# Second layer's expert weights: spread over partitions by transfers from memory, with rings of four buffers

## The reference, cut to what matters

```
combine[t, e] = routed weight of expert e for token t (8 of 64 are non-zero)
routed = sum over e of  combine[t, e] * ( relu(x @ up_w[e])^2 @ down_w[e] )     # 64 experts, 128 -> 64 -> 128
shared = relu(x @ shared_up_w)^2 @ shared_down_w                                # 128 -> 256 -> 128
out    = routed + shared
```

## Time and profile before

| | |
|---|---|
| median of 3 runs | 4811.27 us (4810.74 to 4814.55) |
| profiled execution, its own time | 4804.09 us |
| its span, first to last instruction | 4802.3 us |
| share of the span PE is busy | 76% |
| experts' phase of the second layer, first matmul to last sum | 2185.4 to 2784.8 us |

### The profile page before, as it was taken

The page is one execution under the profiler, slowest core; times in us unless marked ns, Lnnn a source line. Parts: engine busy times, 40 slices in busy tenths (PEclk is TensorE's granted clock), DMA queues, the critical chain, the costliest instruction groups (busy, mean ns, idle before and its releaser), DMA issues. The chain is left out here.

```text
span 4802.3 us, 104516 instructions
## 1 busy us (share of the span) xinstructions
PE 3656.9 (76%) x36852; PEld 2186.3 (46%) x36852; DVE 2650.2 (55%) x5988; ACT 1930.0 (40%) x3735; POOL 1159.8 (24%) x1804
## 2 busy tenths in 40 slices
PE   4699999489956999519999933456447539999997
PEld 1244444257732222216666621135446426666665
DVE  5577777511145777465555564743443546666664
ACT  4366666223323777312222212221102235655553
POOL 0111111000000111004656621600001524444441
PEclk9799999679977999759999966566557859999999
DMA  3322222000003111000000001011000323333331
GB/s 99 72 58 56 57 56 55 6 9 14 5 14 67 46 45 45 4 1 16 13 15 15 15 22 45 30 57 30 4 4 3 53 75 115 114 111 115 116 116 31
DMA packets 179869, 219.27 MB, mean 46 GB/s; under 512 B 36509, under 2 KB 154852, under 8 KB 179182
## 3 DMA queue, kind: packets, MB, share of 16 engines
q1 hardware_dynamic: 175470, 206.76, 15.0%
q0 software_dynamic: 4096, 8.40, 1.2%
HBM read 162.16 MB, written 34.60 MB: 41 GB/s over the span
## 5 line engine op out<-in xcount | busy, mean ns | idle before, releaser
L716 DVE TENSOR_REDUCE att_mx<-att_pS 128x1 f32<-128x512 f32 (+4 forms) x960 | 730.5, 787 | 289.9 <-PE att_pS L587 187.2
L679 ACT ACTIVATE att_E<-att_pX,att_gs 128x512 f32<-128x512 f32 (+3 forms) x1024 | 723.3, 740 | 409.6 <-PE att_pX L613 176.8
L582 PE MATMUL att_pS<-att_ks,att_qs 72*128 72x512 bf16 (+4 forms) x1536 | 409.3, 339 | 80.9 <-DMA att_ks<-parts 57.6
L1841 POOL TENSOR_TENSOR att_E<-att_E,att_rz 128x128 f32<-128x128 f32 (+3 forms) x512 | 357.5, 719 | 437.3 <-DVE att_rz L2049 437.3
L607 PE MATMUL att_pX<-att_qs,att_ks 75*128 75x512 bf16 (+4 forms) x1536 | 421.3, 329 | 30.4 <-ACT att_E L679 15.5
L1533 POOL TENSOR_TENSOR pairs_h<-pairs_c,pairs_r 128x512 f32<-128x512 f32 x272 | 344.2, 1269 | 189.8 <-DVE pairs_c L1593 189.3
L1580 ACT ACTIVATE pairs_r<-pairs_ph 128x512 f32<-128x512 f32 x272 | 162.5, 597 | 437.1 <-PE pairs_pc L1551 435.5
L1593 DVE TENSOR_TENSOR pairs_c<-pairs_pc,pairs_r 128x512 f32<-128x512 f32 x272 | 188.2, 692 | 253.2 <-ACT pairs_r L1580 248.8
L624 PE MATMUL att_pO<-att_E,att_vs 128*9 128x512 f32 (+3 forms) x3072 | 322.4, 492 | 1.3 <-ACT att_E L679 1.3
L545 POOL CAST att_mp<-att_m 16x128 bf16<-16x128 f32 x288 | 80.5, 279 | 942.0 <-DVE att_m L727 916.8
L1559 PEld LDWEIGHTS pairs_po<-pairs_a,pairs_h 128*128 128x128 f32 x2176 | 285.8, 192 | 41.2 <-POOL pairs_h L1533 2.2
(11 more groups left out here) (423 smaller groups left out, 6745.6 us busy)
## 6 DMA issues: line engine op xcount, KB each, us to landing
att_bias<-in_bias_dram SPq DMA_DIRECT2D x64, 896.0 KB, 4.5
parts<-proj_part SPq DMA_DIRECT2D x144, 128.0 KB, 2.3
att_xb<-xnT SPq DMA_DIRECT2D x64, 256.0 KB, 2.7
att_qs<-parts SPq DMA_DIRECT2D x192, 64.0 KB
att_ks<-parts SPq DMA_DIRECT2D x192, 64.0 KB
att_w<-in_w3a_dram SPq DMA_DIRECT2D x64, 192.0 KB, 2.4
att_qs<-parts SPq DMA_DIRECT2D x96, 96.0 KB
att_ks<-parts SPq DMA_DIRECT2D x96, 96.0 KB
```

Source lines behind the costliest of these rows:

```text
L582: ins = nc.tensor.matmul(pS[:, bank, n * w:(n + 1) * w], qs[:K1, u, x, q * P:(q + 1) * P], ks[:K1, u, x, :w], start=(n == 0 or not causal) ...
L679: nc.scalar.activation(E[:, kt % 2, WIDE * xp:WIDE * (xp + 1), :w], places(c)[0], ACT.Exp, scale=gs[:, g % 2, gain_of:gain_of + 1]).then_i ...
L716: V.reduce_max(dst, src, AX.X).then_inc(s_mx, 1)
L1841: nc.gpsimd.tensor_tensor(E[:, k, :width(j)], E[:, k, :width(j)], rz[:, u, k:k + 1].broadcast_to([P, width(j)]), ALU.mult).then_inc(s_n, 1)
```

## The change

A new phase, `spread_phase`, takes the place of "one1", "turn1a" and "turn1b". It turns `comb` itself in float32, copies it to on-chip memory with ACT, and writes it to a table in memory, `cT`: 68 rows of 4096 tokens, row e the weight of expert e, and four rows of ones for the shared part. `pairs_phase` then loads, for each pair, the row of its first expert onto partitions 0 to 63 and the row of its second onto 64 to 127, in two transfers: each reads one row of 16 KB 64 times and is 1 MB at its destination. The table `sel` and its cast, `cA`, `cB` and the two bf16 matmuls are gone. DVE computes `m` = relu(`ph`) * `c` in one instruction with `ph` from PSUM and `c` from the loaded rows, and POOL `h` = `m` * `r`. The rings `ph`, `po`, `r`, `m` and `h` have four buffers, and PE and DVE run three iterations ahead instead of two. SP issues four transfers for a pair, and PE and DVE wait for all four at the pair's first block.

```diff
+def spread_phase(nc, R, name, comb, NE, cT):
+    ROWS = cT.shape[0]
+        wt = p.sb("wt", [ROWS, B * T])
+        pt = p.ps("pt", [P, 2, T])
+            @block.sync
+            def _(sp):
+                sp.wait_ge(s_one, 1)
+                sp.dma_start(cT[NE:, :], wt[NE:, :]).then_inc(s_out, 16)
+                for n in range(B):
+                    sp.wait_ge(s_wt, n + 1)
+                    sp.dma_start(cT[:NE, n * T:(n + 1) * T], wt[:NE, n * T:(n + 1) * T]).then_inc(s_out, 16)
+                sp.wait_ge(s_out, 16 * (B + 1))
+            @block.vector
+            def _(dve):
+                nc.vector.memset(wt[NE:, :], 1.0).then_inc(s_one, 1)
+                nc.vector.memset(R.f[:, :, :], 0.0)
+            @block.tensor
+            def _(pe):
+                for n in range(B):
+                    if n >= 2:
+                        pe.wait_ge(s_wt, n - 1)
+                    for q in range(QT):
+                        ins = nc.tensor.transpose(pt[:NE, n % 2, q * P:(q + 1) * P], comb[:, n * QT + q], R.ident[:, :])
+                    ins.then_inc(s_t, 1)
+            @block.scalar
+            def _(act):
+                for n in range(B):
+                    act.wait_ge(s_t, n + 1)
+                    nc.scalar.activation(wt[:NE, n * T:(n + 1) * T], pt[:NE, n % 2], ACT.Copy).then_inc(s_wt, 1)
...
+    RING, AHEAD = 4, 3
...
-                        for k, src in enumerate((w1, w2, sel)):
-                            dst = a[:, v, k] if k < 2 else a[:, v, 2:].rearrange("p k f -> p (k f)")
-                            sp.dma_start(dst, src[bass.ds(e, 1), :, :].rearrange("o p f -> (o p) f")).then_inc(s_w[v], 16)
+                        for k, src in enumerate((w1, w2)):
+                            sp.dma_start(a[:, v, k], src[bass.ds(e, 1), :, :].rearrange("o p f -> (o p) f")).then_inc(s_w[v], 16)
+                        for k in range(2):
+                            sp.dma_start(c[k * HALF_P:(k + 1) * HALF_P, v], cT[bass.ds(e * 2 + k, 1), :].broadcast_to([HALF_P, B * T])).then_inc(s_w[v], 16)
...
-                        nc.gpsimd.tensor_tensor(h[:, g % 2], c[:, g % 2], r[:, g % 2], ALU.mult).then_inc(s_h, 1)
+                        nc.gpsimd.tensor_tensor(h[:, g % RING], m[:, g % RING], r[:, g % RING], ALU.mult).then_inc(s_h, 1)
...
-                        nc.tensor.matmul(ph[:, g % 2], a[:, v, 0], R.xnT[:, b * T:(b + 1) * T], start=True, stop=True)
-                        nc.tensor.matmul(pc[:, g % 2], sb_[:, v, 0], cA[:, b * T:(b + 1) * T], start=True, stop=False)
-                        nc.tensor.matmul(pc[:, g % 2], sb_[:NC, v, 1], cB[:, b * T:(b + 1) * T], start=False, stop=True).then_inc(s_up, 1)
+                        if b == 0:
+                            pe.wait_ge(s_w[v], at(64, 64 * (g // IT + 1)))
+                        if not (first and g < RING):
+                            pe.wait_ge(s_r, at(IT, g + 1 - RING))
+                            pe.wait_ge(s_m, at(IT, g + 1 - RING))
+                        nc.tensor.matmul(ph[:, g % RING], a[:, v, 0], R.xnT[:, b * T:(b + 1) * T], start=True, stop=True).then_inc(s_up, 1)
...
-                        nc.vector.tensor_tensor(c[:, g % 2], pc[:, g % 2], r[:, g % 2], ALU.mult).then_inc(s_c, 1)
+                        nc.vector.scalar_tensor_tensor(out=m[:, g % RING], in0=ph[:, g % RING], scalar=0.0, in1=c[:, v, b * T:(b + 1) * T],
+                                                       op0=ALU.max, op1=ALU.mult).then_inc(s_m, 1)
```

More of the change, by code:

```diff
@@ L1487, in pairs_phase @@
+def pairs_phase(nc, R, name, NPAIR, w1, w2, cT):
+    RING, AHEAD = 4, 3
+    HALF_P = P // 2
+    with phase(nc, name) as p:
+        a = p.sb("a", [P, 2, 2, P])
+        c = p.sb("c", [P, 2, B * T])
+        r = p.sb("r", [P, RING, T])
+        m = p.sb("m", [P, RING, T])
+        h = p.sb("h", [P, RING, T])
+        ph = p.ps("ph", [P, RING, T])
+        po = p.ps("po", [P, RING, T])
         s_w = [p.sem("w0"), p.sem("w1")]
-        s_sel = p.sem("sel")
         s_up = p.sem("up")
         s_r = p.sem("r")
-        s_c = p.sem("c")
+        s_m = p.sem("m")
@@ L1515, in body @@
                     at = At(pool, i)
[L1517 to L1524, removed]
-                    for g in range(IT):
[L1526 to L1532, removed]
-                        nc.gpsimd.tensor_tensor(h[:, g % 2], c[:, g % 2], r[:, g % 2], ALU.mult).then_inc(s_h, 1)
+                    for g in range(IT):
+                        pool.wait_ge(s_r, at(IT, g + 1))
+                        pool.wait_ge(s_m, at(IT, g + 1))
+                        if not (first and g < RING):
+                            pool.wait_ge(s_o, at(IT, g + 1 - RING))
+                        nc.gpsimd.tensor_tensor(h[:, g % RING], m[:, g % RING], r[:, g % RING], ALU.mult).then_inc(s_h, 1)
                 run_bodies(pool, NBODY, body)
@@ L1555, in down @@
                         pe.wait_ge(s_h, at(IT, g + 1))
-                        if not (first and g < 2):
-                            pe.wait_ge(s_f, at(IT, g - 1))
+                        if not (first and g < RING):
+                            pe.wait_ge(s_f, at(IT, g + 1 - RING))
                         for q in range(QT):
-                            ins = nc.tensor.matmul(po[:, g % 2, q * P:(q + 1) * P], h[:, g % 2, q * P:(q + 1) * P], a[:, v, 1], start=True, stop=True)
+                            ins = nc.tensor.matmul(po[:, g % RING, q * P:(q + 1) * P], h[:, g % RING, q * P:(q + 1) * P], a[:, v, 1], start=True, stop=True)
                         ins.then_inc(s_o, 1)
                     if first:
-                        up(0, True)
-                        up(1, True)
+                        for g in range(AHEAD):
+                            up(g, True)
                     for g in range(IT):
-                        if not (last and g + 2 >= IT):
-                            up(g + 2, first)
+                        if not (last and g + AHEAD >= IT):
+                            up(g + AHEAD, first)
                         down(g, first)
@@ L1577, in body @@
                         act.wait_ge(s_up, at(IT, g + 1))
-                        if not (first and g < 2):
-                            act.wait_ge(s_h, at(IT, g - 1))
-                        nc.scalar.activation(r[:, g % 2], ph[:, g % 2], ACT.Relu).then_inc(s_r, 1)
+                        if not (first and g < RING):
+                            act.wait_ge(s_h, at(IT, g + 1 - RING))
+                        nc.scalar.activation(r[:, g % RING], ph[:, g % RING], ACT.Relu).then_inc(s_r, 1)
                 run_bodies(act, NBODY, body)
@@ L1598, in add @@
                         dve.wait_ge(s_o, at(IT, g + 1))
-                        nc.vector.tensor_tensor(f, po[:, g % 2], f, ALU.add).then_inc(s_f, 1)
+                        nc.vector.tensor_tensor(f, po[:, g % RING], f, ALU.add).then_inc(s_f, 1)
                     if first:
-                        hidden(0, True)
-                        hidden(1, True)
+                        for g in range(AHEAD):
+                            hidden(g, True)
                     for g in range(IT):
-                        if not (last and g + 2 >= IT):
-                            hidden(g + 2, first)
+                        if not (last and g + AHEAD >= IT):
+                            hidden(g + AHEAD, first)
                         add(g)
@@ L1613, in layer1_gate @@
     with ExitStack() as ctx:
[L1614 to L1621, removed]
+        lg = ctx.enter_context(nc.sbuf_tensor("lg1", [P, NT, 64], F32))
+        comb = ctx.enter_context(nc.sbuf_tensor("comb", [P, NT, 64], F32))
+        cT = nc.dram_tensor("weights1", (68, B * T), F32).ap()
         logits_phase(nc, R, "lg_1", t["rw1"], t["rb1"], 64, lg)
         route_phase(nc, R, "route", lg, (t["cbias"], t["lower8"]), comb)
[L1624 to L1642, removed]
+        spread_phase(nc, R, "spread", comb, 64, cT)
+        pairs_phase(nc, R, "pairs", 34, t["up1"], t["down1"], cT)
 def layer2_gate(nc, R, t, moe):
@@ L3184, in layout @@
     t["down1"] = np.concatenate([inp["L1_ffn_down_w"].reshape(32, P, D), inp["L1_ffn_shared_down_w"].reshape(2, P, D)])
[L3186 to L3191, removed]
     t["gw2"], t["gb2"] = f(inp["L2_ffn_gate_w"]), f(inp["L2_ffn_gate_b"][:, None])
```

29 lines of the change are left out of this document (12 added, 17 removed).

## The result

The changed kernel takes 4890.11 us (median of 4 runs, 4885.87 to 4895.6), the one before 4811.01: a ratio of 1.0165, with a 95% interval of 1.0147 to 1.0182. It is slower by 79 us, where the prediction said 4893 and +81.3. The profiled execution took 4890.31 us, its span is 4888.5.

The account below looks back on a forecast made before the run. PE bounds the kernel, but would wait for each pair's slow spreading transfers: +95.7 (experts' phase) - 24.3 (spread phase) + 9.9 (first load) = +81.3, 4885.4, or 4893 as median. Likeliest case's range 4845 to 4945; eight in ten 4670 to 4990.

Parts of the forecast that it names:

- Pace: Experts' phase: without the bf16 matmuls an iteration takes PE 1.75 us instead of 2.19, 119.7 us less over 272.
- The room for the transfers: Experts' phase: from a buffer's release to its next use, 8.57 us remain for a pair's loads, where 12.96 were before.
- The rate: Spreading transfers to 64 partitions each: 222 GB/s, so a pair's 2 MB take 9.45 us; bounds 434 and 47 GB/s.
- Landing: A pair's spread weights land 13.6 us after the buffer's release (1.18 + 2.97 + 9.45), so PE waits 5.0 us.
- Cycle: Experts' phase: time from one pair to the next, 19.03 us, or 20.73 with the clock's loss; before 17.5.
- Clock: Experts' phase: PE runs 3.3 us at half clock after each pause, costing 1.7 us per pair.
- The phase: Whole experts' phase: two pairs of 14.0 us and 32 cycles of 20.73 make 691.4 against 595.7, +95.7 us.
- Spread phase and first load: Before the experts: the new spread phase saves 24.3 us; the wait for the first pair's load adds 9.9.
- the full rate: Rival: the half-partition loads run at full rate and land 8.98 us after release; -125.6 us, 4686; chance 0.20.

Follow-up runs that it names:

- ahead_2: The changed kernel with PE and DVE running two iterations ahead instead of three: 4787.6 us, ratio 0.9970 to the kernel before.
- early_release: The changed kernel with a pair's spreading transfers issued once DVE has last read the buffer, ahead of the weights: 4673.5 us, ratio 0.9734 to the kernel before.
- The two tests: The changed kernel with one row loaded to 128 partitions, and with 64 different rows loaded to each 64 partitions: ratios 0.9716 and 1.0192 to the kernel before.
- kept_busy: The changed kernel with five repeated float32 up-matmuls on PE before it waits for a pair's weights: 4810.5 us, ratio 1.0018 to the kernel before.
- wide_one_row: The changed kernel with one transfer filling all 128 partitions from the first expert's row (wrong weights for the second): 4665.8 us, ratio 0.9716 to the kernel before.
- even_odd: The changed kernel with a pair's hidden rows interleaved, so one transfer fills 128 partitions from two rows: 4670.4 us, ratio 0.9724 to the kernel before.
- two_queues: The changed kernel with ACT issuing the upper half's row in its own queue, beside SP's: 4877.2 us, ratio 1.0155 to the kernel before.

## Why the prediction was right

The steps in its own order, with what the traces show:

- **Pace.** 1.75 us was forecast, 1.75 measured in every kernel here. `m` takes 692 ns, not the 765 of the nearest row; it costs what the instruction before it did, and either lies under PE.
- **The room for the transfers.** Before, no transfer held PE up after the first pair, since 256 KB landed 1.7 to 2.5 us after issue and had 12.96. The step that decided was to work out the room (five iterations less 0.18, 8.57 us) and to see that running further ahead shrinks it. Kernels with another room behave as the formula says: `ahead_2` gave an iteration back (its other 1.3 us are clock), `early_release` removed the wait.
- **The rate.** 222 GB/s was taken from a load to 24 partitions; 221 was measured. This was the uncertain term, with 434 and 47 as its bounds. The two tests show that a half of the partitions, with one row repeated or with 64 different ones, has half of the rate, as the Trainium skill's page (SBUF — State Buffer, "Door 1: The DMA port swizzle") says. They do not show that the 24-partition row was slow for this reason. In it the DMA engines were 69% busy, 20 GB/s for each busy engine; in the change they are fully busy at 13, where the wide load has 27. So the row agreed with the new transfers in its rate and not in what the engines did, and that 222 met 221 is in part luck. The Trainium skill's 218, which the prediction set beside the sum and did not use in it, had the better ground.
- **Landing.** 13.6 forecast, 13.48 measured. **Cycle.** 20.73 and 20.61.
- **Clock.** 1.7 per pair forecast; measured 1.6 by `kept_busy`, and 1.8 as the time from a pair's first up-matmul to the next release (7.18 us, full clock 5.42). The size was right, but the ground was weaker than it looked: the prediction held a pause half as long to be enough, from another phase, and `ahead_2`, with 2.4 to 3.1 us, lost 0.36 us per cycle (17.34 against 16.98 = 2 x 1.75 + 0.18 + 13.30).
- **The phase.** From the first up-matmul to the end of the last `down`: 598.6 before, 692.0 after (by the matmuls' times), +93.4, where +95.7 was forecast: 691.4 was nearly met, and the time before had been taken 2.9 us too short (272 iterations alone, 595.7, without the phase's start and end).
- **Spread phase and first load.** From the end of `comb` to SP's first issue: 2145.50 to 2181.86, 36.4 us, before, and 2142.14 to 2156.21, 14.1 us, after: -22.3 (forecast -24.3). What was mis-sized is SP's pace: its nine issues to the table took 6.3 us (2147.37 to 2153.71), not 4.5, and they began 0.9 us later after routing than assumed; landing and barrier then took 2.5 us, not 3.2. From there to the first matmul 3.5 and 12.9: +9.4 (forecast +9.9). The saving is real, 12.9 us in sum, and lies under the loss.

93.4 - 12.9 = +80.5, against the forecast's +81.3. The spans differ by 86.2; the other 5.7 lie in phases that the change does not touch (one of them alone is 10 us longer, see the last section), and nothing in the prediction spoke of them. So the agreement of the whole within 2 us of 79 is closer than the parts are sure.

Of the rivals, the full rate is what `wide_one_row` and `even_odd` measured. It was priced at -125.6 us; they give about -136 and -132 (ratios 0.9716 and 0.9724 of 4802). The step that was off there is the landing, 7.1 and 7.4 us from issue in place of 7.8, which leaves a wait of 0.1 to 0.2 us per pair where 0.41 was priced.

## What to carry to other kernels

A transfer that is hidden today has a room, from the release of its buffer to its next use; before it grows, work the room out, and remember that each iteration an engine runs ahead is taken from it. Release a buffer at its own last reader, not at the last reader of what is loaded along with it. Spread data to all 128 partitions in one transfer, by interleaving what belongs to two halves, rather than half by half; and where the tensor engine must wait in every round, count the half clock after the pause, which here was a quarter of the loss of each cycle over its work; but look in the trace whether it comes, since pauses of 2.4 to 3.1 us mostly passed without it here.

## What was not expected of the hardware

- Reading one 16 KB row of memory 128 times in one transfer went at the same rate as different rows: 438 GB/s.
- Useless matmuls during a wait made the kernel faster by some 70 us of 4880; 52 us of it are the clock.
- The loss by the clock does not go with the length of the pause alone: 1.8 us per pair after pauses of 4.7 us, 2.3 after 3.9 (`two_queues`), 0.4 after 2.8 (`ahead_2`), while half clock follows stops of 2.4 to 2.9 in another phase.
- A phase of the third layer that no kernel here changes (`chunks_phase`, 10304 matmuls in small pieces) took between 336.5 and 360.7 us in the profiled executions:

```profile
3289.80:3640.20 350.40, 170.36 (x10304) 156.74 (x10304) 159.32 (x289) 36.07 (x64) 0.00 (x0) 0.52 0.02 4
```

```profile
3369.20:3729.90 360.70, 171.60 (x10304) 157.66 (x10304) 159.24 (x289) 36.20 (x65) 0.15 (x1) 0.51 0.02 4
```

```profile
3309.20:3645.70 336.50, 168.89 (x10304) 155.75 (x10304) 159.36 (x289) 36.06 (x64) 0.00 (x0) 0.52 0.02 4
```

These are the kernel before, the changed one and `kept_busy`. The number of matmuls, the busy times and the clock are the same to 1 or 2%, the length differs by 24 us. The difference lies in PE's idle time that the profile puts down to nothing it shows ("issue"), in the two matmul groups of the phase; in the kernel before

```profile
PE chunks_pQ L2375 <- issue: 70.5, 39, 2.5
PE chunks_pK L2375 <- issue: 62.1, 37, 2.2
```

are 132.6 us, and the same two are 142.5 in the changed kernel and 120.2 in `kept_busy`. This is 10 us of the change's 86 in the spans, and more than `kept_busy` gained beyond its cycles. Each is one execution, and the cause stays open; so differences of ten microseconds between kernels of this program should be read from the phase in question, not from the whole time alone.
